# Projections of an attention stage moved: the first block's into the feed-forward block ahead, the second's into the attention's own stream

## What is computed

```python
x = x + 0.5 * _L0_ffn_ref(_layernorm(x))
x = x + _L0_attn_ref(_layernorm(x))
x = x + 0.5 * _L0_ffn_ref(_layernorm(x))
x = x + 0.5 * _L1_ffn_ref(_layernorm(x))   # 8 experts, hidden 128, top 4 picked
x = x + _L1_attn_ref(_layernorm(x))        # 16 heads of 16, causal, ALiBi
x = x + 0.5 * _L1_ffn_ref(_layernorm(x))

# inside _L1_attn_ref
c_kv = hidden_states @ w_dkv.T
q = (hidden_states @ w_q.T).reshape(B, S, HEADS, HEAD_DIM)
k = (c_kv @ w_uk.T).reshape(B, S, HEADS, HEAD_DIM)
v = (c_kv @ w_uv.T).reshape(B, S, HEADS, HEAD_DIM)
scores = jnp.einsum('bqhd,bkhd->bhqk', q, k) * scale + alibi_bias(S)
out = jnp.einsum('bhqk,bkhd->bqhd', jax.nn.softmax(scores, axis=-1), v)
return out.reshape(B, S, HIDDEN) @ w_o.T
```

## Time and profile before

| | us |
|---|---|
| median of three runs | 534.08 (532.31 to 534.10) |
| the profiled execution | 532.84 |
| its span, first to last instruction | 531.1 |
| TensorE busy | 497.2 (94%) |
| VectorE busy | 384.8 (72%) |
| ScalarE busy | 252.4 (48%) |
| GpSimd busy | 109.6 (21%) |
| mean granted TensorE clock | 0.982 |

### The profile page before, as it was taken

One profiled execution on the slowest core, in us unless ns is written; L12 is line 12 of the kernel. 1 busy time (PEld: TensorE's weight loads), 2 busy tenths in 40 slices (PEclk: granted clock), 3 DMA queues, 4 the chain that ended last, 5 costly groups with the idle time before them and its releaser, 6 DMA issues.

```text
span 531.1 us, 9082 instructions
## 1 busy us (share of the span) xinstructions
PE 497.2 (94%) x3074; PEld 422.9 (80%) x3074; DVE 384.8 (72%) x1196; ACT 252.4 (48%) x539; POOL 109.6 (21%) x170
## 2 busy tenths in 40 slices
PE   2999999999999999999999997899789989799996
PEld 1788888888888888888888886788667878678885
DVE  4669787674687674688588787878767878648776
ACT  3657643525323525324574237456445766644441
POOL 1001000110010110010002005637403333414352
PEclk9999999999999999999999999899997999899999
DMA  6432320000000000001200000276488430000011
GB/s 206 118 90 68 97 56 1 1 1 1 2 0 1 1 1 1 1 1 41 60 21 0 2 1 2 91 81 118 150 187 269 111 79 3 1 2 1 3 38 41
DMA packets 18797, 25.87 MB, mean 49 GB/s; under 512 B 2848, under 2 KB 12832, under 8 KB 18752
## 3 DMA queue, kind: packets, MB, share of 16 engines
q1 hardware_dynamic: 17696, 24.78, 17.8%
q10 hardware_dynamic: 1056, 0.51, 0.3%
HBM read 17.42 MB, written 5.24 MB: 43 GB/s over the span
## 4 chain that ended last, share of the span: by engine, by line
PE 79%; DVE 9%; issue 4%; ACT 3%; POOL 2%; SPq 2%; DMA 1%; DVEq 0%; ACTq 0%; POOLq 0%
PE ps L579 22%; PE ps L581 21%; PE ps L580 21%; DVE x L1590 3%; PE ps L908 2%; PE ps L860 2%; PE ps L594 2%; PE ps L891 2%; PE ps L981 1%; DVE ps L1673 1%; POOL al L523 1%; PE ps L872 1%; PE ps L889 1%; ACT z L1013 1%; PE ps L970 1%
## 5 line engine op out<-in xcount | busy, mean ns | idle before, releaser
L579 PE MATMUL ps<-zh,w0u_h 128*128 128x512 f32 x256 | 103.1, 403 | 1.5 <-ACT zh L1020 1.5
L581 PE MATMUL ps<-zl,w0u_h 128*128 128x512 f32 x256 | 102.3, 400 | 0.0
L580 PE MATMUL ps<-zh,w0u_l 128*128 128x512 f32 x256 | 102.1, 399 | 0.0
L1042 ACT ACTIVATE gel<-ps 128x512 f32<-128x512 f32 x64 | 38.2, 597 | 104.4 <-PE ps L581 104.3
L1408 DVE TENSOR_TENSOR act<-gel,ps 128x512 f32<-128x512 f32 x64 | 43.7, 683 | 42.4 <-ACT gel L1042 42.2
L579 PE MATMUL ps<-w0d_h,ah 128*128 128x256 f32 x256 | 73.0, 285 | 0.4
L581 PE MATMUL ps<-w0d_l,ah 128*128 128x256 f32 x256 | 71.5, 279 | 0.0
L580 PE MATMUL ps<-w0d_h,al 128*128 128x256 f32 x256 | 71.4, 279 | 0.0
L1048 ACT ACTIVATE ah<-act 128x512 fp32r<-128x512 f32 x64 | 40.2, 629 | 40.3 <-DVE act L1408 40.3
L1590 DVE SCALAR_TENSOR_TENSOR x<-ps,aff,x 128x256 f32<-128x256 f32 x128 | 53.0, 476 | 8.9 <-PE ps L581 7.1
L579 PEld LDWEIGHTS ps<-zh,w0u_h 128*128 128x128 f32 x256 | 48.7, 190 | 12.8 <-ACT zh L1020 1.8
(11 more groups left out here) (182 smaller groups left out, 1039.7 us busy)
## 6 DMA issues: line engine op xcount, KB each, us to landing
stage<-in_w_dram SPq DMA_DIRECT2D x16, 384.0 KB, 3.0
qs<-split_out SPq DMA_DIRECT2D x24, 128.0 KB, 3.0
ks<-split_out SPq DMA_DIRECT2D x48, 64.0 KB, 2.9
stage<-in_w_dram SPq DMA_DIRECT2D x8, 256.0 KB, 2.7
ks<-pad SPq DMA_DIRECT2D x6, 256.0 KB, 9.7
ks<-pad SPq DMA_DIRECT2D x1, 1024.0 KB, 8.8
split_out<-qh SPq DMA_DIRECT2D x4, 256.0 KB, 2.6
split_out<-ql SPq DMA_DIRECT2D x4, 256.0 KB, 3.0
```

The costliest lines, as they stand in the source:

```text
L579: pe.matmul(o, lh, rh, start=start, stop=False, **kw)
L580: pe.matmul(o, ll, rh, start=False, stop=False, **kw)
L581: return pe.matmul(o, lh, rl, start=False, stop=stop, **kw)
L1042: nc.scalar.activation(gel[:, n % 2, :], ps[:, 2 * (n % 2), :], ACT.Gelu_apprx_tanh).then_inc(gelu_s, 1)
```

## The change

For the first block, transposes, c, q and k move into units 4 to 7 of the feed-forward stage's second block (the rule `hosts_attn1`); for that the layernorm is prepared in unit 1, the weights are rounded after unit 0 and their low parts taken in units 0 to 3. The two transposed parts and the first block's k get places of their own inside the not yet filled stack `qs` (`zh2`, `zl2`, `kh[0]`, `kl[0]`), and the feed-forward block writes "up" into two banks in place of three. The second block's transposes, c, q and k move into steps 8 to 20 of the stream; `project_v(1)` goes to step 1. SyncE's queue reads the first group as soon as three of the four writes are issued, and loads `wa` as soon as the stage before has done its last "down".

```diff
+V0_STEP = 1
+Z1_STEP, C1_STEP, K10_STEP, Q11_STEP, K11_STEP = 8, 11, 14, 17, 20
...
-        kh, kl = ah, al
+        zh2, zl2 = [qs[:, i:i + 4, :].rearrange("p (c s) q -> p c (s q)", c=KC) for i in (0, 4)]
+        kh, kl = [[qs[:, i:i + 4, :].rearrange("p (m s) q -> p m (s q)", m=2), t] for i, t in ((8, ah), (12, al))]
...
+        def hosts_attn1(st, b):
+            return st.kind == "ffn1" and st.after == "attn1" and b == 1
+
         def prepare_at(st, b):
-            return 5 if b == 0 else 4
+            return 1 if hosts_attn1(st, b) else 5 if b == 0 else 4
+
+        def up_bank(n):
+            return n % 2 if "attn1" in stages and n // U1 == blocks_before_attn1 - 1 else n % 3
+
+        def zt_bank(p, kc):
+            return {attn1_p: (2, 3), attn1_p + 1: (PV_BANK, OUT_BANK)}.get(p, (0, 1))[kc]
+
+        def split_z(p):
+            return (zh2, zl2) if p == attn1_p else (zh, zl)
...
             if "attn1" in stages:
-                for b in range(2):
-                    sp.wait_ge(x_s[b], last_ffn0 + 1)
+                sp.wait_ge(down_s, U0 * f0)
                 sp.dma_start(wa_raw, wa).then_inc(wa_s, 16)
...
-                for m, kind in ((0, 0), (1, 0), (0, 1), (1, 1)):
+                for m, kind in ((0, 0), (0, 1), (1, 0)):
                     write(0, m, kind)
-                for h in range(4):
+                read(0)
+                write(0, 1, 1)
+                for h in range(1, 4):
                     read(h)
...
                         if n >= 3:
-                            pe.wait_ge(ah1_s, n - 2)
+                            pe.wait_ge(ah1_s, n - 1 if hosts_attn1(st, b) else n - 2)
...
+                        host = hosts_attn1(st, b)
+                        if host and c == 4:
+                            transposes(attn1_p)
+                        if host and c == 5:
+                            pe.wait_ge(wal_s, WL)
+                            split_ready(attn1_p)
+                            project_c(0)
+                        if host and c == 6:
+                            project_k(0, 0)
+                        if host and c == 7:
+                            project_k(0, 1)
                         if c >= LAG:
                             down1(n - LAG)
+                        if host and c == 5:
+                            project_q(0, 0)
+                        if host and c == 6:
+                            project_q(0, 1)
...
             def attn1(st):
                 p = st.p
                 block_start(st, 0)
-                pe.wait_ge(wal_s, WL)
-                split_ready(p)
-                project_c(0)
-                project_q(0, 0)
-                project_q(0, 1)
-                project_k(0, 0)
+                project_v(0)
                 pe.wait_ge(acc_s, E * f0 + U1 * st.d1 - 1)
-                project_k(0, 1)
-                transposes(p + 1)
-                project_v(0)
-                project_v(1)
-                split_ready(p + 1)
-                project_c(1)
-                project_q(1, 0)
                 for s in range(4 * HEADS + SUM):
...
+                    if s == Z1_STEP:
+                        transposes(p + 1)
+                    if s == C1_STEP:
+                        split_ready(p + 1)
+                        project_c(1)
+                        project_q(1, 0)
+                    if s == K10_STEP:
+                        project_k(1, 0)
+                    if s == Q11_STEP:
+                        project_q(1, 1)
+                    if s == K11_STEP:
+                        project_k(1, 1)
```

More of the change, by code:

```diff
@@ L584, in transposes @@
                 pe.wait_ge(z_s, p + 1)
[L585 to L589, removed]
+                if p == attn1_p:
+                    pe.wait_ge(tk, TK * routed["ffn1", blocks_before_attn1 - 1] + 1)
                 if p == 0:
@@ L626, in block_start @@
                     pe.wait_ge(ah1_s, units(st, b, "ffn1"))
-                if before(st, b) != "attn1":
+                if before(st, b) != "attn1" and st.kind != "attn1":
                     transposes(norm(st, b))
@@ L800, in project_q @@
             def project_q(b, m):
-                if b and m == 0:
-                    pe.wait_ge(v_s, 2)
+                if m:
+                    for done in (kh_s, kl_s) if b else (qh_s, ql_s):
+                        pe.wait_ge(done, 3 if b else 1)
+                z_hi, z_lo = split_z(attn1_p + b)
                 for kc in range(KC):
                     w = W_Q + kc * D + m * P
-                    mm = split3(ps[:, q_bank(b, m), :], wa_h[:, w:w + P], wa_l[:, w:w + P], zh[:, kc, :], zl[:, kc, :],
+                    mm = split3(ps[:, q_bank(b, m), :], wa_h[:, w:w + P], wa_l[:, w:w + P], z_hi[:, kc, :], z_lo[:, kc, :],
                                 kc == 0, kc == KC - 1)
@@ L820, in project_k @@
                 pe.wait_ge(cl_s, b + 1)
-                if b and m == 0:
-                    pe.wait_ge(kh_s, 2)
-                    pe.wait_ge(kl_s, 2)
+                if b:
+                    pe.wait_ge(qh_s, 3 + m)
+                    pe.wait_ge(ql_s, 3 + m)
+                elif m:
+                    pe.wait_ge(kh_s, 1)
+                    pe.wait_ge(kl_s, 1)
                 w = W_K + m * P
@@ L851, in scores @@
                         pe.wait_ge(stack_s[h % HALVES], STACKED * (h // HALVES + 1))
-                    if gp == 0:
-                        for done in (kh_s, kl_s):
-                            pe.wait_ge(done, 2)
                     if gp >= 2:
@@ L1108, in ffn1 @@
                             logits_t_out(routed["ffn1", fb], 3)
+                        host = hosts_attn1(st, b)
+                        if host and c == 6:
+                            q_hi(0, 0)
+                        if host and c == 7:
+                            q_hi(0, 1)
                         act.wait_ge(h1_s, n + 1)
@@ L1127, in ffn1 @@
                             normalise(p + b + 1)
-                        if fb == 1 and c == 2 and "attn1" in stages:
+                        if host and c == 0:
                             act.wait_ge(wa_s, 16)
                             nc.scalar.activation(wa_h[:, :], wa_raw, ACT.Copy).then_inc(wah_s, 1)
-                        if fb == 1 and c == 4 and "attn1" in stages:
+                        if host and c == 1:
                             act.wait_ge(sel_in_s, 32)
@@ L1181, in attn1 @@
                                 out_hi(n, t)
+                    if s == Z1_STEP - 4:
+                        normalise(p + 1)
                     if s % GROUP == 1 and GROUP < s < 4 * HEADS + GROUP:
@@ L1187, in attn1 @@
                         normalise(p + 2)
+                    if s == V0_STEP + 1:
+                        v_out(1)
+                    if s == Z1_STEP + 1:
+                        z_hi(p + 1)
+                    if s == C1_STEP + 1:
+                        c_hi(1)
+                        q_hi(1, 0)
+                    if s == K10_STEP + 1:
+                        k_hi(1, 0)
+                    if s == Q11_STEP + 1:
+                        q_hi(1, 1)
+                    if s == K11_STEP + 1:
+                        k_hi(1, 1)
                     if s > SUM and (s - SUM) % GROUP == 1:
@@ L1551, in ffn1 @@
                                 out_lo(3, 1)
+                        host = hosts_attn1(st, b)
                         if c < 2:
                             left_acc(st, b, 2 - c)
+                        if host and c == 1:
+                            prepare(attn1_p, 0)
                         if c >= 3:
                             acc1(n - 3)
+                        if host and c == 4:
+                            z_lo(attn1_p)
+                        if host and c == 5:
+                            c_lo(0)
+                        if host and c in (6, 7):
+                            q_lo(0, c - 6)
+                            k_lo(0, c - 6)
                         if c == 1 and after_attn1:
@@ L1568, in ffn1 @@
                         first = prepare_at(st, b)
-                        if c == first or c == first + 1:
+                        if not host and c in (first, first + 1):
                             prepare(p + b + 1, c - first)
@@ L1619, in attn1 @@
                 left_acc(st, 0, 3)
-                z_lo(p)
                 left_acc(st, 0, 2)
```

116 lines of the change are left out of this document (49 added, 67 removed).

## The result

The changed kernel took 537.65 us (median of four runs, 537.35 to 539.68); the kernel before, run beside it, 533.22. The ratio on record is 1.0105, 95% interval 1.0078 to 1.0132 (the quotient of the two medians is 1.0083): about 1% slower. The forecast was 531.4, the range up to 535.5. The profiled execution took 537.35 us, its span 535.6 against 531.1, 4.5 us more. TensorE did the same 3074 matmuls and was busy 497.8 us (before 497.2): the same work, later.

A forecast was written before the change was run, and what follows sets the result against it. TensorE bounds the kernel (79% of the ending chain), through waits and clock. Head 0 8.4 us earlier, less 6.8 in steps 7 to 21 and 0.2 at head 32, gives 1.4 off 532.84: 531.4, range 527.3 to 535.5.

The forecast's parts named there:

- The work: Steps 7 to 21 of the stream: no matmul removed, 6.4 us moved in, 17.1 us in all at full clock.
- The host block: Feed-forward's second block: 5.6 us more TensorE work and 0.8 us of waits; last "down" ends at 379.8.
- From there to head 0: Entry to the stream: the stack lands at 381.9, head 0's turned scores come at 388.8, 8.4 us earlier.
- The hand-overs: Steps 7 to 21: 1.9 us waiting between transposes and c at full clock, none at half; three later ones 0.5.
- The clock: Steps 7 to 21: half clock loses 3.4 us, the same as before, with bounds 0 and 5.
- half clock through the loaded steps: Rival, steps 7 to 21: 17.1 us of work take up to 34.2, time up to 544.4; chance 0.07.
- the first rival: Steps 7 to 21: the clock holds or falls only in the thin steps; 529.7, or 527.3 with hand-overs hidden; chance 0.31.
- Head 32: Before head 32's scores: 0.0 to 1.5 us of new wait for the queue's writes and reads, taken as 0.2.
- Any difference of more than 1 us outside 349 to 425: Sign of being wrong: the timeline changes by more than 1 us anywhere outside that stretch.
- The terms costed at nothing: Earlier weight load, two banks for "up" in place of three, and the pad's earlier spread: no cost.

The follow-up runs named there:

- both edits: The changed kernel with the second block's copies first in their step and seven added matmuls in steps 1 to 7: 528.28 us, ratio 0.9906.
- e2_second_only: The kernel before with only the second block's transposes, c, q and k moved into steps 8 to 20 of the stream: 542.33 us, ratio 1.0167.
- e7_z_front: The changed kernel with only the copies of the second block's transposes (zh, zl) first in step 9: 531.54 us, ratio 0.9979.
- e4_fill: The changed kernel with one added 128x128 by 128x512 matmul in each of steps 1 to 7: 532.73 us, ratio 0.9999.

## Why the prediction was wrong

- **The work**: right in kind, a little too high in size. No matmul was removed, and 6.4 us of work came into steps 7 to 21. With both edits these steps took 18.0 with 1.70 of waits, so 16.3 of work where the prediction counted 17.1. Its account of the kernel before closed although 0.67 of waiting there (for VectorE, at 398.76) was left out, so its step was a little too long.
- **The host block**: right. The last "down" starts at 379.00 (forecast 378.4), z made the moved transposes wait 0.37 (0.3), and no wait for `al` or `wa_l` shows. The 0.7 us by which the block started later lie ahead of the moved work. In the kernels with the copies in front and with the added matmuls, which have the same instructions up to there, the block's own transposes start at 343.48 and 343.67, so I count it as spread.
- **From there to head 0**: right, 8.6 for 8.4. The first scores came at 382.83 (381.9), the turned ones at 389.28 (388.8).
- **The hand-overs**: this step failed. "1.9 of waiting at full clock, none at half; the three later ones are even, 0.5 in all". The waits were 2.89 from head 0 to head 14 and 1.06 behind it, 3.95 in all (0.67 in the kernel before). The prediction gave z's chain 4.3 us from the end of the transposes, and counted the half clock as time that hides it. The chain itself took less, 2.9 us from the shift at 394.13 to the end of z's low part at 397.05, but it began 1.9 us after the transposes' end: the copy stood last in its step, behind work that waits for later TensorE matmuls, and these ran at half clock, so half clock did not hide the hand-over but lengthened it. And only the stretch to head 14 was looked at: k's last copy is in step 21, and the stop at 417.6 lies behind head 14, in a stretch that lost 2.8 us and to which the prediction gave 0.
- **The clock**: 3.4 lost was forecast, once. The first period was as forecast, 6.8 us long. Two more followed, behind stops, and the sum had no term for them. The prediction weighed one idle stretch without a fall; the kernel before also has one with a fall, at the second block's transposes, where the granted clock is 1.00 at 380 to 382 and 0.50 at 384 to 386:

```profile
382.68 1.88 PE L594 MATMUL ps<-ident,z 128*128 128x128 f32 x8 [2.65 <-ACT z L1013]
...
384.00:386.00 2.00, 2.00 (x11) 2.00 (x10) 1.38 (x2) 1.06 (x3) 0.00 (x0) 0.50 1.01 321
```

- **The rivals**: "half clock through the loaded steps" got 0.07 and was to decide from 15 us of half clock in steps 7 to 21 on. It did not come in that form: 8.4 us lay in those steps and 3.4 behind them, and the clock cost 2.5 us more than forecast while the waits cost 3.4 more. Head 14's turned scores, at 413.07, are behind the 412 that the prediction itself named as a sign of being wrong. The kernel with the copies in front lands at 529.76, beside the first rival's 529.7, but with the clock still falling once; that the numbers agree is chance.
- **The rule of the Trainium skill** ("TensorE: Matmul & The Clock Gate", Part 1, activity releases the throttled clock) bears on the added matmuls: with more activity in the thin steps the granted clock was 1.00 at 388 to 390 in place of 0.50, and 4.9 us came back; this trace agrees. In the kernel before, eight such matmuls brought no gain that is shown.
- **Head 32**: right within its 0.2. SyncE's reads of its group start at 417.22, and TensorE did not wait:

```profile
417.22 1.39 SPq L429 DMA_DIRECT2D qs<-split_out  x3
```

- **"Any difference of more than 1 us outside 349 to 425"**: there was none. The terms costed at nothing (the earlier load of the weights, two banks for "up") were not taken back one by one; no wait for either shows in the trace.

## What to carry to other kernels

Work moved into a busy loop needs its copies costed by their place in the other engines' lists, not by their durations: a copy that stands behind work which waits for the mover's next matmuls is late by that whole round. Putting the copies first gave 7.9 us here, with one new wait of 0.99 us, for VectorE's minimum behind k's low part. Before moving filler out of a wait, ask what the wait will be filled with; each half of this change alone was slower than the kernel before, and neither was faster than the whole change. And look behind each stop of TensorE for a fall of the clock, which can cost as much again: 3.4 us at half clock, 1.7 lost, followed each stop for z, while the stop of 1.06 us for nmin had a fall behind it in two kernels (the changed one and e2_second_only) and none in two others (e7_z_front, e4_fill).

## What had not been expected

- Work that does nothing paid: seven matmuls, 1.6 us at full clock, took 4.9 us off the changed kernel.
- The fall of the clock came late. In the changed kernel TensorE was busy 0.69 of 2.0 us at 384 to 386 with a granted clock of 1.00, and 1.92 of 2.0 at 388 to 390 with 0.50. The period struck the work that stands behind the thin stretch.
- Runs of one kernel differ by their clock: twelve runs with the copies in front went from 528.26 at a mean granted clock of 0.989 to 534.87 at 0.982. As an estimate, 0.007 of some 530 us of span is 3.7 of the 6.6 us between them. With the added matmuls as well, six went from 526.74 to 529.45, at 0.992 to 0.995.
